# Layer 0 of 24 of 32 images computed inside the attention stage, in a form without ScalarE

## The reference, cut to what matters

```python
def _L0_conv_ref(inp, W2, b2, W3, b3, beta2, beta3):        # 32 images, 64 channels, 56 x 56
    x = inp.reshape(B, G, CPG, H, Wd)                        # 8 groups of 8 channels
    p2 = x[:, :, _I2] * x[:, :, _J2]                         # 36 products of two channels of a group
    y2 = einsum('bgihw,goi->bgohw', p2, W2) + b2
    p3 = x[:, :, _I3] * x[:, :, _J3] * x[:, :, _K3]          # 120 products of three
    y3 = einsum('bgihw,goi->bgohw', p3, W3) + b3
    return inp + y2 * beta2 + y3 * beta3 * CONV3_SCALE

def _L1_conv_ref(l, ...):
    g = clip(_bn(conv1x1(l, w_inside)), 0.0, 6.0)
    theta = l[:, :c_red]                                     # 32 channels
    f = einsum('niab,nicd->nabcd', theta, theta)             # 3136 x 3136 scores per image
    f = softmax(f, over the first pair of axes)
    f = softmax(f, over the second pair of axes)
    out = einsum('nabcd,nicd->niab', f, g)
    out = _bn(conv3x3_depthwise(out / h * w)) + l
```

## Time and profile before

| | |
|---|---|
| median of 3 runs | 5233.37 us (5229.21 to 5234.2) |
| profiled execution, first to last instruction (span) | 5229.7 us |
| busy: TensorE | 5201.4 us |
| busy: ScalarE | 5093.6 us |
| busy: GpSimd | 4435.3 us |
| busy: VectorE | 4411.4 us |

### The profile page before, as it was taken

One profiled execution on the slowest core, in us unless ns is written; L12 is line 12 of the kernel. 1 busy time (PEld: TensorE's weight loads), 2 busy tenths in 40 slices (PEclk: granted clock), 3 DMA queues, 4 the chain that ended last, 5 costly groups with the idle time before them and its releaser, 6 DMA issues.

```text
span 5229.7 us, 88157 instructions
## 1 busy us (share of the span) xinstructions
PE 5201.4 (99%) x32196; PEld 2524.0 (48%) x32196; DVE 4411.4 (84%) x8862; ACT 5093.6 (97%) x2949; POOL 4435.3 (85%) x1854
## 2 busy tenths in 40 slices
PE   9999999999999999999999999999999999999999
PEld 3333355444545444545454444545454545444544
DVE  8888888888888888888888888888888888888887
ACT  8888889999999999999999999999999999999998
POOL 7666655998888998888998998899888899888988
PEclk9999999999999999999999999999999999999999
DMA  8898852223222222223232223222222322222122
GB/s 161 169 185 168 164 104 46 48 55 64 55 63 54 55 63 63 63 63 63 63 63 54 47 52 64 59 61 60 48 60 63 63 63 63 63 63 55 43 42 49
DMA packets 226669, 380.19 MB, mean 73 GB/s; under 512 B 158086, under 2 KB 174527, under 8 KB 216128
## 3 DMA queue, kind: packets, MB, share of 16 engines
q1 hardware_dynamic: 225136, 373.67, 34.5%
q10 hardware_dynamic: 1104, 0.89, 0.1%
HBM read 258.82 MB, written 102.74 MB: 69 GB/s over the span
## 4 chain that ended last, share of the span: by engine, by line
PE 83%; ACT 10%; issue 5%; DVE 2%; DMA 0%; SPq 0%; POOL 0%; DVEq 0%
PE at_AV L1302 35%; PE at_S L1261 21%; PE at_AV L1308 10%; ACT at_ring L1044 7%; PE l_TY L612 6%; PE l_TY L619 4%; PE l_SEL L601 3%; ACT at_ring L1050 3%; PE at_AV L1298 2%; DVE at_ring L1117 2%; PE at_AV L1273 0%; DVE at_GT L1177 0%; DVE at_ZACC L1220 0%; DMA l_X<-in_x 0%; DVE at_ACC L1210 0%
## 5 line engine op out<-in xcount | busy, mean ns | idle before, releaser
L1117 DVE TENSOR_SCALAR_CACHE_REDUCE at_ring<-at_S 128x1344 f32<-128x1344 f32 (+2 forms) x2352 | 2882.8, 1242 | 461.2 <-PE at_S L1261 444.3
L992 POOL TENSOR_TENSOR at_ZP<-at_ZP,at_ring 128x1568 f32<-128x1568 f32 x640 | 2268.5, 3581 | 144.4 <-ACT at_ring L1050 134.4
L1302 PE MATMUL at_AV<-at_ring,at_GT 128*64 128x392 f32 x12800 | 2300.3, 500 | 3.8 <-issue 3.7
L1044 ACT ACTIVATE at_ring<-at_ring,at_NM 128x3136 f32<-128x3136 f32 x784 | 2272.6, 2899 | 12.8 <-DVE at_NM L1126 11.8
L1050 ACT ACTIVATE at_ring<-at_ring,at_RZ 128x3136 f32<-128x3136 f32 x784 | 2274.0, 2901 | 0.0
L1302 PEld LDWEIGHTS at_AV<-at_ring,at_GT 128*64 128x64 f32 x12800 | 854.1, 137 | 1143.8 <-issue 1107.6
L1261 PE MATMUL at_S<-at_THM,at_THS 128*128 128x448 f32 x5376 | 1381.7, 387 | 11.6 <-DVE at_ring L1117 9.2
L1261 PEld LDWEIGHTS at_S<-at_THM,at_THS 128*128 128x128 f32 x5376 | 927.1, 188 | 631.6 <-DVE at_ring L1117 291.4
L1013 POOL TENSOR_TENSOR at_OUTB<-at_OUTB,at_ZB 128x1568 f32<-128x1568 f32 x246 | 878.1, 3570 | 16.8
L1308 PE MATMUL at_AV<-at_ring,at_ones 128*32 128x392 f32 x7168 | 676.9, 498 | 2.9 <-DVE at_ACC L1210 2.9
L567 DVE TENSOR_TENSOR l_U<-l_TY,l_XB 128x512 f32<-128x512 f32 x784 | 486.8, 683 | 86.0 <-PE l_TY L612 84.3
(11 more groups left out here) (91 smaller groups left out, 2491.4 us busy)
## 6 DMA issues: line engine op xcount, KB each, us to landing
at_THM<-hld SPq DMA_DIRECT2D x128, 392.0 KB, 6.2
at_THS<-hld SPq DMA_DIRECT2D x256, 192.0 KB, 4.0
l_X<-in_x SPq DMA_DIRECT2D x124, 392.0 KB, 7.2
at_CIN<-att SPq DMA_DIRECT2D x62, 406.0 KB, 7.5
at_ZB<-rzd SPq DMA_DIRECT2D x62, 406.0 KB, 7.8
yd<-l_YO SPq DMA_DIRECT2D x128, 196.0 KB, 5.4
att<-at_ACC SPq DMA_DIRECT2D x248, 98.0 KB
at_OUTB<-yd SPq DMA_DIRECT2D x62, 392.0 KB, 8.5
```

Source lines behind the costliest of these rows:

```text
L992: e.tensor_tensor(z, z, v, ALU.add).then_inc(g_add, 1)
L1044: e.activation(v, v, ACT.Exp, bias=NM[:, i:i + 1], accum_out=ZS[:, i:i + 1]).then_inc(a_p1, 1)
L1117: e.tensor_scalar(ring[:, s % RING, SC * a_:SC * b].rearrange("p (b w) -> p b w", w=SC), PS[:, k % 2, bank:bank + b - a_, 0:SC], 1.0, None ...
L1302: ins = e.matmul(dst[64 * j:64 * j + 64, 0:QC], GT[fl.n % 2][:, keys_of(fl.n, t), :], ring[:, slot, q:q + QC], start=(i == 0), stop=(i == ...
```

## The change: what it does

Only the first 8 images go through the old layer 0 (49 steps instead of 196). The other 24 are computed inside attention, by 7 steps of 448 pixels an image, 168 in all, in this form: SyncE loads channel products' factors several times over into `XI` and `XJ` (`pair_in`, five DMAs, 0.80 MB) and another factor into `XB` (`factor_in`, four DMAs, 0.92 MB); GpSimd multiplies `XI` by `XJ` (`product`, 896 elements a partition); TensorE multiplies by weights (`products`: eight matmuls of 32 rows by 64 columns of the array, into one score slot and one `at_AV` bank); VectorE multiplies by the other factor (`outer` for three banks, 1344 elements, and `evacuate` for the fourth, 448); TensorE sums (`sums`, four matmuls of 448 columns), VectorE adds the bias, and SyncE stores `YO`. After seven steps GpSimd splits the image's first 32 channels (`split`) and SyncE stores them.

Besides: the ring has 9 tiles and is freed by halves; GpSimd sums 12 tiles of an image instead of 11; the 31 instructions of line 1002 are gone (their term is folded into the first product of the convolution); `YT` is one buffer instead of two; SyncE's due times come from the planner's clock.

```diff
-SPARE = 1.6
+SPARE = 1.4
+AHEAD = 1.0
+MOVED = 24
+MARGIN = 30
...
-RING = 10
+RING = 9
...
-POOL_OF = (2, 2, 2, 2, 2, 1, 0)
+POOL_OF = (3, 2, 2, 2, 2, 1, 0)
...
+def paces(n_img):
+
+
+    gap = (base(n_img - 1) - NT - MARGIN) / (SPLIT * MOVED) if MOVED else 0
+    return {CT * n + u: int(gap * (SPLIT * n + u)) for n in range(MOVED) for u in range(CT)}
...
             l0_sync, l0_gpsimd, l0_scalar, l0_vector, l0_tensor, l0_stored, l0_multiplied, l0_closed = layer0(
-                nc, ctx, memory, a, x, yd, hld, n_img)
+                nc, ctx, memory, a, x, yd, hld, first_moved)
...
+            def pair_in(k):
+                n, w = of_step(k)
+                if k:
+                    e.wait_ge(pe_f, fill_of("t", k - 1) + 1)
...
+                for t in range(2):
+                    e.dma_start(XI[:, t, :], x[n, 32 * t:32 * t + 32, w].unsqueeze(1).broadcast_to([32, 4, SC])).then_inc(s_pair, 16)
+                for d, src in ((1, x), (2, xs[2]), (3, xs[3])):
+                    e.dma_start(XJ[d:128:4, :, :], src[n, :, w].rearrange("(t c) w -> c t w", t=2)).then_inc(s_pair, 16)
+
+            def factor_in(k):
+                n, w = of_step(k)
+                if k % CT:
+                    e.wait_ge(pe_f, fill_of("y", k - 1) + 1)
+                elif k:
+                    e.wait_ge(s_hl2, 128 * (k // CT))
+                for r in range(4):
+                    e.dma_start(XB[:, r, :], xs[4][n, 16 * r:16 * r + 16, w].unsqueeze(1).broadcast_to([16, 8, SC])).then_inc(s_fac, 16)
...
+            def product(k):
+                e.wait_ge(s_pair, 80 * (k + 1))
+                e.tensor_tensor(XI[:, :, :], XI[:, :, :], XJ[:, :, :], ALU.mult).then_inc(g_p2, 1)
+
+            def split(m):
+                e.wait_ge(s_th2, 64 * (m + 1))
+                e.tensor_copy(HO.bitcast(F32R), TH).then_inc(g_h2, 1)
+                e.wait_ge(g_h2, 2 * m + 1)
+                e.tensor_tensor(TH.bitcast(F32R), TH, HO, ALU.subtract).then_inc(g_h2, 1)
...
-                elif step == 1:
-                    e.wait_ge(s_ob, 32 * (n + 1))
-                    link(e.tensor_scalar(OUTB[:, :], OUTB[:, :], 1.0, bq[:, 4:5], ALU.mult, ALU.add))
...
-                if s >= RING and c == 0:
+                if s >= RING:
                     for n, u in tiles_of(s - RING):
-                        e.wait_ge(pe_f, index["z", n, group_of(u), 1] + 1)
-                        if u in POOLED:
-                            e.wait_ge(g_add, added(n, u, 1))
+                        for h in halves(m, n, n_img):
+                            e.wait_ge(pe_f, index["z", n, group_of(u), h] + 1)
+                            if u in POOLED:
+                                e.wait_ge(g_add, added(n, u, h))
...
+            def outer(k):
+                e.wait_ge(pe_f, fill_of("t", k) + 1)
+                e.wait_ge(s_fac, 64 * (k + 1))
+                e.scalar_tensor_tensor(out=XB[:, 0:3, :], in0=PS[:, p.step_slot[k] % 2, :, 0:SC], scalar=RD[:, 32:33], in1=XB[:, 0:3, :],
+                                       op0=ALU.add, op1=ALU.mult).then_inc(v_u, 1)
...
+            def products(f, k):
+                q = p.step_slot[k]
+                if k == 0:
+                    e.wait_ge(v_w2, 5)
+                e.wait_ge(g_p2, k + 1)
+                drained(e, q - 2)
+                e.wait_ge(v_ev, f - 1)
+                for t in range(2):
+                    for r in range(4):
+                        bank = PS[64 * t:64 * t + 64, q % 2, r, 0:SC] if r < 3 else AV[f % 2][64 * t:64 * t + 64, 0:SC]
+                        ins = e.matmul(bank, WT2[32 * r:32 * r + 32, t, :], XI[32 * r:32 * r + 32, t, :], start=True, stop=True)
+                ins.then_inc(pe_f, 1)
+
+            def sums(f, k):
+                e.wait_ge(v_u, k + 1)
+                e.wait_ge(v_ev, max(f - 1, fill_of("t", k) + 1))
+                for r in range(4):
+                    ins = e.matmul(AV[f % 2][32 * r:32 * r + 32, 0:SC], RD[:, 0:32], XB[:, r, :], start=True, stop=True)
+                ins.then_inc(pe_f, 1)
```

More of the change, by code:

```diff
@@ L135, in group_of, with halves, block_of @@
     return next(g for g, r in enumerate(GROUPS) if t in r)
-def batch_of(t):
-    return next(b for b, r in enumerate(BATCHES) if t in r)
+def halves(m, n, n_img):
+    return (0, 1) if n == n_img - 1 or SC * piece(m)[2] > HW // 2 else (0,)
+def block_of(n, n_img, p, j):
+    return 4 * j + p if n == n_img - 1 else 2 * p + j
 class Fill:
@@ L162, in plan @@
     n_buf = scored(total)
+    steps = CT * MOVED
+    first_moved = n_img - MOVED
+    pace = paces(n_img)
+    p = Plan()
+    fills, ended, at = p.fills, p.ended, p.at
     pre, main = [], []
     for n in range(n_img):
-        for b, r in enumerate(BATCHES):
+        for b in range(len(BATCHES)):
             f = base(n) - NT + 6 + 4 * b
-            pre.append(Fill("g", n, b, 0, f + 3 * (n == 1) if n else 2, f + 4 + 3 * (n == 1) if n else 4, n_img))
+            pre.append(Fill("g", n, b, 0, f if n else 2, f + 4 if n else 4, n_img))
@@ L323, in plan @@
                 n, t_, h = adds.pop(0)
-                tg = end_add[n, t_, h] = t + (1700 if t_ == POOLED[0] else 3600)
-                pool.append(("add", (n, t_), h))
+                tg = end_add[n, t_, h] = t + (1520 if t_ == POOLED[0] else 3590)
+                p.pool.append(("add", (n, t_), h))
+            elif what == "prod":
+                tg = end_p[n_p] = t + 2100
+                p.pool.append(("prod", n_p, 0))
+                n_p += 1
+            elif what == "split":
+                tg = end_split[n_h] = t + 2800
+                p.pool.append(("split", n_h, 0))
+                n_h += 1
             else:
                 n, step = conv.pop(0)
-                tg = t + (3600 if step == 0 or step % 2 and step > 1 else 1620)
-                pool.append(("conv", n, step))
-    return pe, dve, pool, fills, ended, max(tp, ta, td, tg)
+                tg = t + (3580 if step == 0 or step % 2 and step > 1 else 1600)
+                if step == 19:
+                    conv_end[n] = tg
+                p.pool.append(("conv", n, step))
+    for k in range(steps):
+        at["pair", k] = pair_issue(k)
+        at["factor", k] = factor_issue(k)
+    for k in range(steps):
+        at["y", k] = closed[k]
+    for n in range(n_img):
+        at["thm", n] = thm_issue(n)
+        at["thl", n] = thl_issue(n)
+        for h in range(2):
+            at["ths", n, h] = ths_issue(n, h)
+        for b in range(len(BATCHES)):
+            at["yt", n, b] = yt_issue(n, b)
+        if n >= first_moved:
+            at["th", n] = closed[CT * (n - first_moved) + CT - 1] + 5000
+            at["held", n] = end_split[n - first_moved]
+        if n < n_img - 1:
+            at["conv", n] = conv_end[n]
+    for k, f in enumerate(fills):
+        at["ev", k] = cleared[k]
+        if f.kind in ("o", "z") and f.i == len(GROUPS) - 1:
+            at["sums", f.n] = max(at.get(("sums", f.n), 0.0), cleared[k])
+    for n in range(n_img - 1):
+        at["loads", n] = max(at["sums", n] + 14000, at["store", n - 1] + 1 if n else 0.0)
+        at["store", n] = conv_end[n] + 10000
+    p.at["span"] = max(tp, ta, td, tg)
+    return p
 def layer0(nc, ctx, memory, a, x, yd, hld, n_img):
@@ L402, in y_use @@
         return 4 * min(u + 2, NU) + u
+    TY = [banks[(i + 3 - y_use(NU - 1)) % 4] for i in range(4)]
     def stored(e):
@@ L461, in sync @@
                 split_out(n - 1)
-            if EARLY <= n < EARLY + 2 * len(early) and (n - EARLY) % 2 == 0:
+            for part in [j for m, j in EARLY if m == n]:
                 for i in range(2):
@@ L465, in sync @@
                     e.wait_ge(s_hl[i], 128)
-                early[(n - EARLY) // 2]()
+                early[part]()
         split_out(n_img - 1)
@@ L728, in build @@
         s_thl = sem("thl")
-        s_yt = [sem(f"yt{i}") for i in range(2)]
+        s_yt = sem("yt")
+        s_w4 = sem("w4")
+        s_pair = sem("pair")
+        s_fac = sem("fac")
+        s_y2 = sem("y2")
+        s_th2 = sem("th2")
+        s_hl2 = sem("hl2")
+        g_one = sem("gone")
+        g_p2 = sem("gp2")
+        g_h2 = sem("gh2")
+        v_u = sem("vu")
+        v_w2 = sem("vw2")
         s_acc = sem("acc")
@@ L1020, in _ @@
                     add(*n, i)
+                elif what == "prod":
+                    product(n)
+                elif what == "split":
+                    split(n)
                 else:
@@ L1238, in _ @@
             acts["lz"] = last_shares
-            for what, *args in dve_order[NP + 1:]:
+            for what, *args in dve_order[NP:]:
                 acts[what](*args)
```

481 lines of the change are left out of this document (350 added, 131 removed).

## The result

| | before | after |
|---|---|---|
| median (lowest to highest) | 5233.01 us (5229.21 to 5234.2) | 5366.63 us (5356.15 to 5367.63) |
| profiled span | 5229.7 us | 5364.4 us |
| first exponential of attention | 724.0 us | 193.7 us |

The ratio is 1.0254 (95% interval 1.0239 to 1.0268): the changed kernel is 2.5% slower. Forecast was 5044 us, so 323 us are missing. Layer 0 gave up what it should: the first `at_ring` exponential stands at 193.7 us, where 193 was forecast, against 724. All of the loss lies in attention, which grew from 4475 us to 5141 (193.7 to 5334.3).

The account below looks back on a forecast made before the run. It took ScalarE and TensorE as equal bounds in attention, with layer 0 at TensorE's pace. Its sum: 5229.7 - 531.0 + 320 + 22 = 5041 us span, 5044 us as median; range 4965 to 5170 us.

Parts of the forecast that it names:

- Layer 0, -531 us: Layer 0: 147 of 196 steps removed at 3.612 us each, all on the path, -531.0 us.
- TensorE's new work, +320 us: Attention: `products` 134, `sums` 129, fewer `z` units -42, more changes of matmul kind 99; +320 us.
- GpSimd's waits, +22 us: Attention, GpSimd: waits of 5.7 us an image for loads, +22 us, within 0 to +141 us.
- The clock: Attention: TensorE's clock was read at its higher level, 2.4 GHz; no term for a lower clock.
- VectorE under cover: Attention, VectorE: 2.79 us more a step, 468 us in all, stays under cover at 88% busy.
- Ring, 12 tiles, one `YT` buffer, at nothing: Attention: smaller ring put at nothing, single `YT` not priced; summing change counted only in the engines' work, -42 us on TensorE.
- SyncE at nothing: Attention: 2472 more DMAs, 1.3 to 2.6 ms of queue, nothing on the path beyond the GpSimd term.
- A: Attention: ScalarE stays the bound, TensorE's visits fall into time not really full; 4703 to 4924 us, chance 0.12.
- C: Attention: `products`' eight tiles run two at a time, 505 instead of 134 us; 5416 us, slower, chance 0.05.
- D: Attention: new steps stretch too far, images not ready when their attention starts; some 5200 us, chance 0.05.
- B: Attention: GpSimd and the DMA queue become the bound, late loads starve ScalarE; 5164 us, chance 0.27.

Follow-up runs that it names:

- e12: The changed kernel with only the planner's assumed time for factor loads raised from 7 to 14 us; 5218.88 us, ratio 0.9974 to the kernel before.
- e1: The changed kernel with no images moved into attention (all 196 layer 0 steps run first), the rest of the change kept; 5275.35 us, ratio 1.0080.
- e8: The changed kernel with the planner assuming 20 us for pair and factor loads and 40 us for the convolution's; 5969.47 us, ratio 1.1412.
- e11: The changed kernel with the planner assuming 20 us for pair loads, 14 for factor loads and 40 for the convolution's; 5747.30 us, ratio 1.0984.
- e16: The changed kernel with only the planner's assumed time for factor loads raised, to 17 us; 5426.14 us, ratio 1.0374.
- e4: The changed kernel with the planner assuming 14 us instead of 7 for pair and factor loads, 30 instead of 20 for the convolution's; 5246.63 us.
- e6: e4 with most of GpSimd's convolution instructions left out for 30 of 32 images; 5233.22 us, ratio 1.0004.

## Why the prediction was wrong

It forecast faster with 0.94, and the kernel is slower. By its own steps:

- Layer 0, -531 us: right. First exponential at 193.7 us.
- TensorE's new work, +320 us: right. Between 800 and 4700 us TensorE is idle for 3900 - 3707 = 193 us, and for 127 us more it is busy at 1.2 GHz (the clock's records laid over its rows). If a matmul takes twice as long there (passes 0.80 against 0.43 us apart), 64 of the 127 are lost. That leaves 3643 us of own work for 592 tiles, an estimate of 6.15 us a tile; forecast 150.8/24.5 = 6.155. `products` 0.94 and `sums` 0.89 us with their visits.
- GpSimd's waits, +22 us, with an upper end of +141: this is the step that failed. "In this static order a GpSimd that runs late finds its data there" held for `ZB` in part (134/24 = 5.6 us an image, 9.8 before) and not for the new pair loads (107 us), so the waits stayed at 10 us an image. Put into the term's own working, that gives (10 - 4.9) x 28.8 = 147 us and 5169 us in all, still faster than before. So the size of the wait isn't what failed most, but what it was weighed against. The term set an engine's waits against its room per image; what counts is each single product against the place of its matmuls. A late GpSimd stops TensorE at the next `products`, and TensorE had no room to make it up: 125 of its 193 idle us stand right ahead of `products`. e12 has none of these waits and is 148 us faster. In its stretch from 800 to 4700 us TensorE is idle for 98 us instead of 193, and busy at 1.2 GHz for 81 instead of 127. Its order differs in other places too, so that all of the 148 us come from this one wait is not shown.
- The clock: priced at nothing. Before, it was at 1.2 GHz for 10 us of the 4300 in the earlier trace rows; after, for 164 us of 3900.
- VectorE under cover: wrong in part, 47 us for the long instruction of `outer` alone.
- Ring, 12 tiles, one `YT` buffer, at nothing: wrong, 43 us (e1).
- SyncE at nothing: not separated. Its queue holds factor loads for 645.6 us behind `sums`, but they are ready when used: VectorE waits 9 us for them.

Together 148 + 43 + 47 = 238 us have a run, of 323 + 22 = 345 us. The remaining 107 us stay open. In e12 TensorE is still idle for 98 us in 3900 and busy at 1.2 GHz for 81 more, against 45 and none in e1. The largest part of the idle time stands ahead of score matmuls, which wait for VectorE: 45.8 + 28.3 = 74 us in e12, and in e1

```profile
PE at_S L1573 <- DVE at_ring L1413: 13.7, 29, 1.1
```

What would free the 45.8 us that stand behind VectorE's copies wasn't tried. That the three parts add up without overlap is assumed.

The rivals: A falls (ScalarE at 87%). C falls: the rows show its eight tiles side by side. D, as "stretches over too much of attention", isn't the changed kernel's (last step at tile 700, forecast 705), but e8, e11 and e16 show that it was one planner constant away, at 207 to 751 us over e12 with no more work. B named the mechanism, loads that come late and a ScalarE that starves, and even so its 5164 us were 203 too low: it priced GpSimd's wait once, and the chain behind it not. B's reason, GpSimd's load, isn't the cause in e4's order (e6); in the changed kernel's it wasn't tried. No rival on the slower side was built on the place of an instruction in a fixed order, and that is where the sign was lost. That the 148 us which e12 gives back and the 147 us of the term's own working are nearly alike is chance: the one is TensorE's time, the other GpSimd's.
